# Local attention normalised ahead across its pairs and into the next stage; feed-forward with a 32-bit router and its first masks made one batch early

## What is computed

```python
x = x + attn_a(layernorm(x))   # causal attention, 32 heads, ALiBi
x = x + ffn(layernorm(x))
x = x + attn_b(layernorm(x))   # 32 query heads, 8 key heads, window of 128, rope
x = x + ffn(layernorm(x))
# ffn: inter = x @ c1.T @ c2.T            router, rank 16, 1792 columns
#      in each block of 32 columns the first largest one is kept
#      h = relu(w1 @ x) where kept, 0 elsewhere;  out = h @ w2t
```

## Time and profile before

| | |
|---|---|
| median of 3 runs | 2882.4 us |
| the profiled execution | 2883.13 us |
| its span, first to last instruction | 2881.4 us |
| first feed-forward, from its first router matmul to the last `add_out` | 585 to 1003 us |
| local attention | 1004 to 2448 us |
| second feed-forward | 2449 to 2881 us |
| mean granted TensorE clock | 0.948 of full speed |

### The profile page before, as it was taken

How to read it: one execution, slowest core, us unless ns; L and a number is a source line. 1 busy time by engine, 2 the same in 40 slices (tenths; PEclk the granted TensorE clock), 3 DMA queues, 4 the chain that set the end, 5 groups by cost and what they waited for, 6 DMA issues and landing times. The chain is left out here.

```text
span 2881.4 us, 41531 instructions
## 1 busy us (share of the span) xinstructions
PE 2615.5 (91%) x14476; PEld 2048.0 (71%) x14476; DVE 1775.2 (62%) x3488; ACT 1311.4 (46%) x2952; POOL 1006.8 (35%) x742
## 2 busy tenths in 40 slices
PE   4788988778988979999999997999999999789899
PEld 2444443456766768888888875888888887567677
DVE  3564655167777656666666646666666664777775
ACT  2354545332211256666665645666666664322221
POOL 2111122154222244444444423444444442452221
PEclk7889998889999999999999999999999999899999
DMA  4334142130000011110001100111001100300000
GB/s 157 100 93 131 48 112 60 37 115 1 1 0 0 11 51 37 37 36 29 30 14 36 37 30 8 38 37 36 29 7 36 36 22 1 115 1 15 15 15 15
DMA packets 114422, 117.42 MB, mean 41 GB/s; under 512 B 7204, under 2 KB 86948, under 8 KB 114276
## 3 DMA queue, kind: packets, MB, share of 16 engines
q1 hardware_dynamic: 113968, 115.77, 13.3%
q10 hardware_dynamic: 340, 0.14, 0.0%
HBM read 92.09 MB, written 22.68 MB: 40 GB/s over the span
## 5 line engine op out<-in xcount | busy, mean ns | idle before, releaser
L1956 POOL TENSOR_TENSOR rope_straight<-rope_straight,rope_crossed 128x512 f32<-128x512 f32 x160 | 207.3, 1296 | 498.9 <-DVE rope_crossed L1736 498.9
L558 POOL TENSOR_TENSOR f_hidden_low<-f_hidden,f_hidden_high 128x512 fp32r<-128x512 f32 x112 | 145.2, 1296 | 523.7 <-ACT f_hidden_high L496 523.7
L1754 DVE TENSOR_TENSOR o_low<-o_sum,o_high 128x512 fp32r<-128x512 f32 x128 | 88.5, 692 | 318.6 <-ACT o_high L1940 318.6
L983 DVE TENSOR_REDUCE a_max<-a_work 128x1 f32<-128x384 f32 (+3 forms) x352 | 204.9, 634 | 109.9 <-PE a_work L871 107.0
L1098 ACT ACTIVATE a_probs<-a_scores 128x512 f32<-128x512 f32 x320 | 173.9, 597 | 160.4 <-PE a_scores L893 84.5
L1843 ACT ACTIVATE probs<-probs,exp_bias 128x256 f32<-128x256 f32 (+1 forms) x512 | 240.2, 470 | 5.6 <-DVE exp_bias L1719 5.5
L1848 ACT ACTIVATE probs<-probs,exp_sum_inverse 128x256 f32<-128x256 f32 (+1 forms) x512 | 205.2, 472 | 32.4 <-DVE exp_sum_inverse L1724 32.4
L1854 ACT CAST q_high<-rope_straight 128x512 fp32r<-128x512 f32 x128 | 79.5, 621 | 292.3 <-POOL rope_straight L1956 292.3
L1564 PE MATMUL w_sum<-o_high,wo_high 128*128 128x512 f32 x512 | 203.5, 397 | 7.5 <-DVE xt L1761 4.7
L1564 PE MATMUL w_sum<-o_high,wo_low 128*128 128x512 f32 x512 | 202.7, 396 | 0.0
L272 PE MATMUL f_hidden_sum<-z_high,f_w_high 128*128 128x512 f32 x448 | 189.2, 422 | 14.0 <-DVE f_hidden L396 14.0
(11 more groups left out here) (258 smaller groups left out, 7636.9 us busy)
## 6 DMA issues: line engine op xcount, KB each, us to landing
a_queries<-a_q_stacked SPq DMA_DIRECT2D x16, 1024.0 KB, 6.3
wq_raw<-in_L_attn_b_wq SPq DMA_DIRECT2D x32, 512.0 KB, 3.7
wo_raw<-in_L_attn_b_wo SPq DMA_DIRECT2D x16, 1024.0 KB, 6.5
a_q_stacked<-a_q_part_high SPq DMA_DIRECT2D x32, 256.0 KB
f_w_raw<-in_L_ffn_w SPq DMA_DIRECT2D x14, 512.0 KB, 10.4
f_w_raw<-in_L_ffn_w2t SPq DMA_DIRECT2D x14, 512.0 KB, 11.2
a_q_stacked<-a_q_part_low SPq DMA_DIRECT2D x16, 256.0 KB
wkv_raw<-in_L_attn_b_wk SPq DMA_DIRECT2D x16, 256.0 KB, 6.5
```

Source lines behind the costliest of these rows:

```text
L558: e.tensor_tensor(hl[:, j % 2], hm[:, :], f32(hh[:, j % 2]), ALU.subtract).then_inc(hl_ready, 1)
L983: e.tensor_reduce(mx[:, t % 2, to:to + nh], bank, AX.X, ALU.max).then_inc(work_free[k], 1)
L1956: e.tensor_tensor(ra[:, slot], ra[:, slot], rb[:, slot], ALU.add).then_inc(roped, 1)
```

## The change

1. **Router in plain 32 bits.** `router` takes 4 matmuls of the unsplit `c1s` and `zf` in place of 12 of split ones, and so waits for `normalise` and not for `high_z` and `low_z`. It moves from the end of the batch to the end of chunk 5; `high_t` and `stack_t` follow it. `zf` is one tile that all stages share.
2. **Masks ahead of the edge.** The scores and masks of chunk 0 of the next batch are made in chunk 6 of this one (`next_scores`, `find_max(... "next I")`), and turned before the last `down`. `up(0)` of a batch now waits for the new `z` tiles. On VectorE `low_z` stands before the second half of these masks.
3. **Layer norm's steps.** `sum_x` moves behind chunk 0, all squares and their sums into chunk 2, `var` to chunk 3, `normalise` to chunk 4. At a stage's start `c2s` is split in two pieces, and the router waits for `c1` alone.
4. **Local attention.** The even batch of the next pair is normalised in the last group of this one, and at the end of pair 1 batch 0 for the second feed-forward, which then starts without a layer norm of its own (`given`). The odd batch of pair 1 is normalised beside the five projections, as pair 0 already does it. Weights for the next pair's first group are loaded and split in the last group.

The diff, cut to its core:

```diff
@@ -117,12 +114,12 @@
-        order = [("I", 0), ("I", 1)]
+        order = []
         for c in range(NCH):
-            order += [("M", c)] + ([("I", 2 * c + 2), ("I", 2 * c + 3)] if c + 1 < NCH else [])
-            order += [("mean", 0)] * (c == 1) + [("var", 0)] * (c == 4)
-        order += [("T", 0)]
-        BEFORE = ["T"] if given else ["mean", "var", "T"]
+            order += [("M", c)] * (c > 0)
+            order += [("I", 2 * c + 2), ("I", 2 * c + 3)] if c + 1 < NCH else [("next I", 0), ("next I", 1), ("next M", 0)]
+            order += [("mean", 0)] * (c == 1) + [("var", 0)] * (c == 3) + [("T", 0)] * (c == 5)
+        BEFORE = [("mean", 0), ("var", 0)] * (not given) + [("T", 0), ("next I", 0), ("next I", 1), ("next M", 0)]
         HALF = len(order) // 2
         LAST = ("I", "M", "mean", "var") if ahead else ("I", "M")
...
-            def router_first(it):
-                e.wait_ge(zh_ready, of_ln(it, DT) + DT)
-                e.wait_ge(zl_ready, of_ln(it, DT) + DT)
+            def router(it):
                 bank, full = aux_write(e, it, "T")
-                for n, (w, z) in enumerate([(c1h, zh), (c1h, zl), (c1l, zh)]):
-                    for d in range(DT):
-                        mm = e.matmul(bank[0:CROWS, :], w[:, d, :], z[:, d, :],
-                                      start=n == 0 and d == 0, stop=n == 2 and d == DT - 1)
+                if it is None:
+                    e.wait_ge(c1_in, 16)
+                for d in range(DT):
+                    if it is None and not given:
+                        e.wait_ge(first_z, d + 1)
+                    elif d == 0:
+                        e.wait_ge(z_ready, of_ln(it, 1) + 1)
+                    mm = e.matmul(bank[0:CROWS, :], c1s[:, d, :], zf[:, d, :], start=d == 0, stop=d == DT - 1)
                 mm.then_inc(full, 1)
...
+            def next_scores(it, half):
+                if half == 0:
+                    aux_done(e, it, "T")
+                    if it is None:
+                        e.wait_ge(c_low, 1)
+                bank, full = aux_write(e, it, "next I", half)
+                scores_of(bank, 0, half).then_inc(full, 1)
...
+                if c:
+                    e.wait_ge(mask_ready, it * 2 * NCH + 2 * c + 2)
+                    bank, full = aux_write(e, it, "M", c)
+                else:
+                    e.wait_ge(mask_ready, 2 if it is None else (it + 1) * 2 * NCH + 2)
+                    bank, full = aux_write(e, it, "next M")
...
             def up(it, j):
                 e.wait_ge(h_masked, it * IT + j + 1)
+                if j == 0:
+                    e.wait_ge(zh_ready, of_ln(it - 1, DT) + DT if not first_batch(it) else DT)
+                    e.wait_ge(zl_ready, of_ln(it - 1, DT) + DT if not first_batch(it) else DT)
...
             def body(it, first, last):
-                router_scores(it, 0)
+                if ahead or not last:
+                    normalised = {1: mean, 3: var}
+                else:
+                    normalised = {}
                 for c in range(NCH):
                     up(it, 2 * c)
                     if c == 0:
-                        up(it, 1)
+                        if first:
+                            up(it, 1)
+                            turn_masks(None, 0)
+                            router_scores(it, 1, 0)
+                        else:
+                            router_scores(it, 1, 0)
+                            up(it, 1)
+                        router_scores(it, 1, 1)
                     else:
-                        if c == 1:
-                            router_scores(it, 1, [1])
                         down(it, 2 * c - 2)
-                    turn_masks(it, c)
-                    if c + 1 < NCH:
-                        router_scores(it, c + 1, [0])
+                        turn_masks(it, c)
+                    if c and c + 1 < NCH:
+                        router_scores(it, c + 1, 0)
+                    elif c and not last:
+                        next_scores(it, 0)
                     if c:
                         up(it, 2 * c + 1)
                         if c + 1 < NCH:
-                            router_scores(it, c + 1, [1])
+                            router_scores(it, c + 1, 1)
+                        elif not last:
+                            next_scores(it, 1)
                         down(it, 2 * c - 1)
-                    if c == 1 and (ahead or not last):
-                        mean(it)
-                    if c == 4 and (ahead or not last):
-                        var(it)
+                    if c in normalised:
+                        normalised[c](it)
+                    if c == 5 and not last:
+                        router(it)
                 down(it, IT - 2)
                 if not last:
-                    router_first(it)
+                    turn_masks(it, 0)
                 down(it, IT - 1)
             e.sem_inc(h_used, 2)
             if not given:
                 first_mean()
                 first_var()
...
                 for c in range(NCH):
-                    if c == 2 and (ahead or not last):
+                    if c == 2 and normal:
                         centre(it)
-                    if c == 5 and (ahead or not last):
+                    if c == 4 and normal:
                         variance(it)
+                    if c + 1 == NCH and not last:
+                        stack_t(it)
                     for half in range(2):
                         keep_hidden(it, 2 * c + half)
+                        if c + 1 == NCH and half == 1 and normal:
+                            low_z(it)
                         if c + 1 < NCH:
                             find_max(it, c + 1, half, chain)
-                    if c == 5 and (ahead or not last):
+                        elif not last:
+                            find_max(it, 0, half, chain, "next I")
+                    if c == 4 and normal:
                         normalise(it, chain)
-                if ahead or not last:
-                    low_z(it)
-                if not last:
-                    stack_t(it)
...
                     if c == 2:
-                        square(it, 0)
-                        square(it, 1)
-                    if c == 3:
-                        square(it, 2)
-                        square(it, 3)
-                    if c == 5:
+                        for d in range(DT):
+                            square(it, d)
+                    if c == 4:
                         seed(it)
+                    if c == 5 and not last:
+                        high_t(it)
                 if ahead or not last:
                     high_z(it)
-                if not last:
-                    high_t(it)
...
-            e.wait_ge(c_in, 32)
-            e.copy(c1h[:, :, :], c1_raw[:, :, :]).then_inc(c_high, 1)
-            e.copy(c2s[:, :], c2_raw[:, :]).then_inc(c_high, 1)
             if not given:
                 seed(None)
+            e.wait_ge(c2_in, 16)
+            for cols in (slice(0, CH), slice(CH, INTER)):
+                e.copy(c2s[:, cols], c2_raw[:, cols]).then_inc(c_high, 1)
...
             def body(it, first, last):
-                if ahead or not last:
-                    sum_x(it, Chain(e, pool_step, it * 2))
                 for c in range(NCH):
                     low_hidden(it, 2 * c)
                     low_hidden(it, 2 * c + 1)
@@ -567,11 +594,11 @@
                         if c + 2 < NCH:
                             low_w1(c + 2)
                         low_w2(c + 1)
+                    if c == 0 and (ahead or not last):
+                        sum_x(it, Chain(e, pool_step, it * 2))
                     if c == 2 and (ahead or not last):
-                        sum_squares(it, 0)
-                    if c == 3 and (ahead or not last):
-                        sum_squares(it, 1)
-                        sum_squares(it, 2)
+                        for n in range(3):
+                            sum_squares(it, n)
...
             rest = slice(64, CROWS)
-            e.tensor_tensor(c2s[rest, :], c2_raw[rest, :], f32(c2s[rest, :]), ALU.subtract).then_inc(c_low, 1)
-            e.wait_ge(c_low, 2)
-            low_w1(0)
-            low_w1(1)
+            for n, cols in enumerate((slice(0, CH), slice(CH, INTER))):
+                e.wait_ge(c_high, n + 1)
+                if n:
+                    e.wait_ge(w1_low, n)
+                e.tensor_tensor(c2s[rest, cols], c2_raw[rest, cols], f32(c2s[rest, cols]), ALU.subtract).then_inc(c_low, 1)
+                e.wait_ge(c_low, n + 1)
+                low_w1(n)
             low_w2(0)
...
             def before(pair):
                 it = pair * KVH - 1
-                if pair == 0:
-                    mean(0, 1)
-                else:
-                    for k in range(2):
-                        e.wait_ge(ring_free[k], pair * KVH * (len(proj) // 2))
-                    e.wait_ge(s_max, pair * (KVH * UNITS * ST))
```

(58 more changed lines are left out.)

244 lines of the change are left out of this document (119 added, 125 removed).

## The result

The changed kernel took **2847.7 us** (median of 4 runs, 2844.25 to 2850.38), the kernel before 2881.8 beside it: a ratio of 0.9877 with a 95% interval of 0.9864 to 0.9891. Timed again later, the ratio was again 0.9877 (0.9860 to 0.9894). The forecast was 2843 in a range of 2822 to 2864. The profiled execution spans 2846.3 us where that of before spans 2881.4, so 35.1 us are to be explained (34.1 by the medians).

What follows compares the result with a forecast made beforehand. TensorE was taken to bound the kernel, busy 2615.5 of 2881.4 us. Terms 23.2 - 3.0 + 3.6 + 8.6 + 7.8 = 40.2 us, off the profiled 2883.1, gave 2843 us, range 2822 to 2864.

Steps and rivals of the forecast that it cites:

- The edges: Six joins between feed-forward batches: warm periods of 97.95 us instead of about 102.2, gaining 23.2 us in all.
- TensorE waits 5.1 us where it waited 5.4: Wait for the next masks before a batch's last down, about as long as the old wait for z_low.
- the cold stretch: down(13) and up(0) behind the new wait run at a lowered clock, costing 1.9 us per edge.
- The last edge: Sixth batch join, taken to be without sum_x: period 96.75 us where it was 98.85, a gain of 2.1.
- The first batches: First batch of each feed-forward call: squares bunched, sums behind weight splits on GpSimd; 1.5 us lost per call, -3.0 (bounds 0, -8).
- Stage starts: Earlier first scores: first feed-forward gains 3.6 us; second gains 7.8, its scores 11.3 us behind the last add_out.
- Pair 0 to pair 1: Local attention: layer norm moved into the last group brings pair 1's first o_sum earlier, gaining 8.6 us (bounds 0, 14).
- The 1.85 that I took off for a cold stretch: Between local attention's pairs: one lowered-clock stretch behind a wait, subtracted from 10.5 us to give 8.6.
- Rival B: Batch edges: masks really ahead, the 5.1 us wait and cold 1.9 vanish at six edges; 42 us, 2801; chance 0.12.
- Rival C: Chunks 1 to 3: find_max slowed to 2.06 from 0.69 by contention, 3.3 us more per period; 2863; chance 0.16.
- Rival D: Behind each 5.1 us wait the clock stays down through five matmul blocks, up to 14 us per edge; 2915; chance 0.03.
- Rival E: Ends of local attention give nothing, ScalarE and VectorE being late in the last group: 16.4 us gone, 2859; chance 0.04.

Runs made afterwards that it cites:

- the swap: Changed kernel, with VectorE making the second half of the next masks ahead of the four low_z in a batch's last chunk; 2809.8 us, ratio 0.9738 to the kernel before.

## Why the prediction was right, and where it was not

It forecast 40.2 us and got 35.1 by the trace, with the mechanism of most steps as it put them.

- **The edges.** The step "TensorE waits 5.1 us where it waited 5.4" was right within 0.15 at all six edges, and so was the place. The window's 91.38 us of busy time, less 1.4 lost to the cold clock (the lower granted one), are 90.0 of hot work, at the full clock, against 89.75; its 5.8 us of idle are the wait and 0.69 at the transposes of chunk 1. Two small terms were too large: the cold stretch costs 1.4 us (transposes 1.03 for 0.62, the `down` behind them 3.94 for 2.98), not 1.9, and `sum_x` 0.3 to 0.7 (waits of 0.42 to 0.88 in chunk 1, 0.16 in the one batch without it), not 1.2. So the period is 97.16 us, in others 97.20, 98.03 and 98.83, against 97.95.
- **The last edge.** I left `sum_x` out of the last period, since before its absence made the difference of 1.92 to 5.42 us. After, `sum_x` runs in chunk 0 of the batch ahead of that edge and is still there: 98.03, not 96.75. The term of 2.1 was 0.5.
- **The first batches: the term that was mis-sized.** The prediction put -3.0 us, 1.5 a call, with -8 as the bound. Against the looped edges' mean of 4.5 us the two first batches fell short by 5.4 and 5.7, 11.1 in all, outside the bound. The mechanism it named was right, and so was its size: the copy came 3.6 us late, two were covered, and TensorE waited 1.55 and 1.14 us. What it had at nothing were the other waits behind the same splits: 0.9 and 1.6 for `centre`, 0.8 once for a mask of chunk 2, 0.5 each for a mask of chunk 4, and 1.6 each for the router, since `normalise`, moved into chunk 4, stands beside the next splits (`keep_hidden(10)` lost 3.9 us there).
- **Stage starts.** 3.6 forecast; by the first scores 591.77 - 586.87 = 4.9, less the 1.2 of an earlier end of causal attention, 3.7. The second: 11.3 us from the last `add_out` to the scores, measured 11.5.
- **Pair 0 to pair 1.** Forecast 8.6, measured 10.2: the wait at `w_sum` 1.96 (2.0 forecast), the variance 3.60, the first turn at 1737.72 behind a projection at 1716.80, 20.9 us (20.7 forecast). The 1.85 that I took off for a cold stretch was in effect counted twice. The clock does fall there, 0.51 between 1742.0 and 1752.5 us, at a wait of TensorE of 6.51 us for `probs_turned_low` (1746.89). But pair 0 of the kernel before has the same wait of 6.51 us, with 0.51 between 1041 and 1048 us, so the stretch lay already in the 39.4 us taken over from there. From the first turn to the first `o_sum` were 40.4.
- **Rival B** is what the swap made true: with the masks ahead in earnest the edges give 35.5 us more (42 forecast for it, the wait of 1.2 that stays being most of the difference). **Rival C** did not happen as written: the only transposes of chunks 1 to 3 that waited near 2 us for masks are chunk 1's in the very first batch (1.84, and 2.11 in the second trace), where before had 2.88, and in the looped batches `f_mask` took 0.95 us at most. What it has in common with the loss of the first batches is GpSimd's work. **Rival D**'s longer cold stretch was not seen, behind 5.09 us or behind 8.29: there `down` took 4.94 us and the `up` after it 2.91 again. **Rival E**'s loss was not there. D's price was also wrong in itself: five blocks of 12 at 4.59 for 2.75 are 9.2 us an edge and not 14, so D would have been about 2887, hardly slower than before. (And 4.2 x 5 + 2.1 is 23.1; 23.2 comes of unrounded terms.)

The rule of the Trainium skill that was weighed (*SBUF — State Buffer*, "SBUF: two separate sides", an exclusive lock) was borne out in kind: four `z_low` take 3.19 us alone and 6.39 beside three sums. At the one place where I had used it as a price, chunk 1 beside `sum_x`, it cost less than I put, 0.3 to 0.7 us and not 1.2, far from the 2.8 of full locking; the price fell in the first batches, where GpSimd has most work.

## What to carry to other kernels

When work is moved ahead of an edge, follow each engine's order to the last wait: here the masks went ahead on TensorE but stood behind four `low_z` on VectorE, and one swap there was worth as much as the whole change (35.5 and 35.1 us by the traces). A schedule that is right for the looped batches has to be priced again for the first one, where weight preparation runs beside it. And two halves that feed the same start (a ready batch, a router that needs no split) may be worth little one by one, so test them together before dropping either; and read such a thing from the place where it is due, since the medians of whole kernels did not show it here.

## What the runs showed of the hardware that I had not expected

- The same VectorE instruction with two SBUF inputs takes 0.69 us alone and 2.02 to 2.06 (`f_mask`) or 2.87 (`f_ln_tmp`) beside a GpSimd split of 128x1024. `f_is_max<-f_aux`, which reads one of its inputs from PSUM, stays at 0.69 in all 112 of the changed kernel, the two beside such a split included. Without the splits chunks 1 to 6 of a first batch last as long as in a looped one, within 0 and 1.6 us.
- At the edges: behind a wait of 1.23 us the window's granted clock was 1.00, behind 5.09 us 0.71, and the price was 1.4 us there and 2.4 behind 8.29: transposes 1.03 in both, `down` 3.94 and 4.94, against 0.62 and 2.98 warm. Longer waits cost more, but for one `down` only. The `up` that follows is warm in both cases (2.91).
- The end of an unchanged stage moved by 6 us between profiled executions, more than most single edits here are worth.
